# A pair's last six stack loads are issued from ScalarE's queue instead of SyncE's

## Chip, core and metric

The kernel runs on one core of a Trainium2 chip. The metric is the device time of one execution in microseconds (us). The core's engines each have an instruction stream of their own and meet only at semaphores: TensorE (PE, with its weight loads PEld), VectorE (DVE), ScalarE (ACT), GpSimd (POOL) and SyncE (SP), which here only issues DMAs. A row marked SPq or ACTq belongs to the instruction queue of that engine: a DMA that it issues, or a wait.

## What is computed

Two layers on x (32 batches, 64 tokens, 256 features). Each layer adds a gated attention and a gated feed-forward part. The time lies almost wholly in the first layer:

```
x = x + tanh(g_xattn[0]) * attention0(layernorm(x), ctx, ctx, mask)   # 8 heads of width 8, 256 x 256 scores, per batch
x = x + tanh(g_ffn[0])   * moe0(layernorm(x))                         # top-p router, 8 experts, 256 -> 512 -> 256, gate * up
x = x + tanh(g_xattn[1]) * attention1(layernorm(x), ctx, mask)        # one head, 64 tokens
x = x + tanh(g_ffn[1])   * moe1(layernorm(x))                         # 4 experts by token position
```

In attention0 a batch's x (64 x 256) is read as 64 channels by 256 positions: q = Wq x, k = Wk ctx, v = Wv ctx, and for each head softmax(q k / sqrt(8) + mask) v.

## The kernel before

The 32 batches are worked in 16 pairs. The main loop has 39 *steps* `n`, of which the first 32 hold the attention of one batch each; even and odd step make a pair `q = n // 2`. A step has eight *half steps* `i`, one for each head, and `g = 8n + i` numbers the heads through. Every engine's program is the same loop written out by hand in that engine's order, and the order in a half step is fixed.

The work of one head `g` runs through all engines. PE multiplies the stacked q and k into the scores (`scores`), DVE adds the mask and finds the row maximum (`maxima`, which ends with `exp_bias`, L1226), ACT takes the exponentials (`exps`, two ACTIVATEs at L701) and cuts them into a high f16 part (`p_high`, L709), POOL makes the low part (`p_low`, L592), SP issues one DMA that transposes both parts (`turn`, L429, into `p_turn`), and PE multiplies the turned parts with v (`times_v`), four half steps after the scores. Between these PE runs the experts of earlier pairs, one expert ("unit") in two half steps: gate matmuls in `psG`, up matmuls in `psU`; ACT takes a tanh of the gate (`unit_tanh`, L725), DVE multiplies, ACT cuts the product (`unit_high`, L731, into `hp_hi`), POOL makes its low part (`h_low`, L584, into `hp_lo`), and PE multiplies both with the down weights into `psY` (`unit_down`), one unit later. In half step 0 of an odd step ACT also turns out the normalised x of a finished pair (`x_high`, L715, into `xT`).

The scores need q and k as *stacks*: three bf16 parts of each, laid out several times over the partitions (`q_stack`, `k_stack`, double buffered by pair). The parts are stored to a scratch tensor in DRAM (`store_parts`, half step 3 of an even step) and read back by twelve DMAs for each pair, three in each of four *pieces*. `load_stacks(eng, par, q, piece)` issues one piece on the queue of the engine that it is given: L343, L348, and L353 or L356. It waits until the parts are stored. All twelve count on one semaphore, for which PE waits before the first scores of the next pair. Before, SP issues pieces 0 and 1 in half steps 6 and 7 of the even step and pieces 2 and 3 in half steps 0 and 1 of the odd step, each behind the turn of that half step. ACT issues pieces 2 and 3 for the very first pair alone, ahead of the loop.

SP's order in a half step is: the turn of head g-1 (which waits for `p_high` and `p_low` of that head), in half step 0 a mask load (L382), then a piece of stack loads where one is due. A turn that is ready is not issued before what stands ahead of it on SP.

Of the kernel before, what the change touches and what calls it, by code (L numbers as in the profile page):

```python
# [42 lines left out]
NPAIR = B * S // P  # L43
# [44 lines left out]
def build(nc, A, out):  # L88
# [5 lines left out]
    def sem(name):  # L94
        return ctx.enter_context(nc.semaphore(name))
# [7 lines left out]
    with ctx:  # L103
# [45 lines left out]
        s = {n: sem(n) for n in names}  # L149
# [183 lines left out]
        def load_stacks(eng, par, q, piece):  # L333

            eng.wait_ge(s["parts_stored"], 16 * (q + 1))
            if q < 2:
                eng.wait_ge(s["stacks_set"], 2)
                eng.wait_ge(s["q_zeroed"], q + 1)
            hh, i = piece // 2, piece % 2
            lo = 64 * hh  # L340
            src = [[part_d[par, w, c].rearrange("(g d r) n -> g d (r n)", g=2, d=DH)[hh]
                    for c in range(3)] for w in range(2)]
            eng.dma_start(  # L343
                q_stack[lo + 24 * i:lo + 24 * i + 24, par, hh, :, :, :].rearrange("r b h n -> r (b h n)"),
                src[0][i].unsqueeze(1).broadcast_to([DH, 3, 2048])
            ).then_inc(s[f"stack{par}_loaded"], 16)

            eng.dma_start(  # L348
                k_stack[lo + 24 * i:lo + 24 * i + 24, par, :, :, :].rearrange("r b h n -> r (b h n)"),
                part_d[par, 1].rearrange("c (g d r) n -> g d c (r n)", g=2, d=DH)[hh]  # L350
            ).then_inc(s[f"stack{par}_loaded"], 16)
            if i == 0:
                eng.dma_start(q_stack[lo + 48:lo + 56, par, hh, :, :, :].rearrange("r b h n -> r (b h n)"),  # L353
                             src[0][2]).then_inc(s[f"stack{par}_loaded"], 16)
            else:
                eng.dma_start(k_stack[lo + 48:lo + 56, par, :, :, :].rearrange("r b h n -> r (b h n)"),  # L356
                             src[1][0]).then_inc(s[f"stack{par}_loaded"], 16)
# [5 lines left out]
        def _(sp):  # L363
# [57 lines left out]
            def turn(g):  # L421

                sem, count = low_done(g)
                sp.wait_ge(s["phi_done"], g + 1)
                sp.wait_ge(sem, count)
                if g >= 4:
                    sp.wait_ge(s["pv_done"], g - 3)
                sem, count = turned(g)
                sp.dma_start(p_turn[:, g % 4, :, :, :, :].rearrange("p a t m n -> p (a t m) n"),  # L429
                             p_parts[:, g % 4, :, :, :].rearrange("p a t m -> p (a t m)"), transpose=True  # L430
                             ).then_inc(sem, 16)

            def step(n):
                q, par = n // 2, n // 2 % 2
                even = n % 2 == 0
                for i in range(8):
                    g = 8 * n + i
                    if 1 <= g <= 8 * B:
                        turn(g - 1)
                    if i == 0 and 1 <= n and n + 1 < B:  # L440
                        sp.wait_ge(s["max_done"], 16 * n)
                        load_mask(n + 1, (n + 1) % 2)
                    if even and i == 3 and 1 <= q and q + 1 < NPAIR:
                        sp.wait_ge(s[f"stack{1 - par}_loaded"], STACK_DMAS * 16 * ((q + 1) // 2))
                        store_parts(1 - par, q + 1)
                    if even and i == 2 and q + 3 < NPAIR:
                        sp.wait_ge(s["v_projected"], q + 2)
                        sp.dma_start(ctx_in[:, 1 - par, :], ctx_d[q + 3]).then_inc(s[f"ctx{1 - par}_loaded"], 16)
                    if even and i >= 6 and q + 1 < NPAIR:
                        sp.wait_ge(s["scores_done"], 8 * n)  # L450
                        load_stacks(sp, 1 - par, q + 1, i - 6)
                    if not even and i < 2 and q + 1 < NPAIR:
                        load_stacks(sp, 1 - par, q + 1, i + 2)
                    if i % 2 == 0 and 6 + g // 2 < 3 * NE:
                        load_weight_stage(6 + g // 2)
                    for t, r in late_at(n, i):
                        if r == 5 and t + 2 < ROUNDS:
                            load_late_ctx(t + 2)
                    out_group = group_at(Y_TURN_AT, g - 1)
                    if out_group is not None:  # L460
                        for tt in range(2):
                            store_out(2 * out_group + tt)
                    if (n, i) in ((TAIL_STEP, 4), (TAIL_STEP + 1, 0)):
                        load_late_weights(n - TAIL_STEP + 2)
                if n == TAIL_STEP - 2:
                    open_late()
                    for t in range(2):
                        load_late_ctx(t)
                if n == TAIL_STEP - 1:
                    for e in range(2):  # L470
                        load_late_weights(e)
# [174 lines left out]
        def _(act):  # L646
# [146 lines left out]
            def late_y_out(k):  # L793

                act.wait_ge(s["down_done"], 2 * (N_UNITS + 2 * k + 2))
                if k:
                    act.wait_ge(s["d_yT"], k)
                for hb in range(2):
                    act.activation(d_yT[:, hb, :].rearrange("p (r q e) -> p r q e", r=4, e=NE1),  # L799
                                   psY[:, hb, :].rearrange("p (e r q) -> p r q e", e=NE1, r=4),  # L800
                                   ACT.Copy, scale=dy_gate[:, 0:1]).then_inc(s["d_yevac"], 1)

            def step(n):
                q, tail = n // 2, tail_pair(n)
                for i in range(8):
                    g, hp, half = 8 * n + i, i // 2, i % 2
                    if 1 <= g <= 8 * B:
                        p_high(g - 1)
                    w = weight_at(g)
                    if w is not None:  # L810
                        w_high(*w)
                    if g < 8 * B:
                        exps(g)
                    k = group_at(Y_OUT_AT, g)
                    if k is not None:
                        late_y_out(k)
                    if half == 0:
                        u0 = unit_at(n, hp, 0)
                        if u0 is not None:
                            unit_tanh(u0)  # L820
                    else:
                        u1 = unit_at(n, hp, 1)
                        if u1 is not None:
                            unit_high(u1)
                    for t, r in late_at(n, i):
                        if r == -1:
                            late_norm(t, 0)
                        elif r == 5:
                            late_norm(t, 1)
                        elif r == 0:  # L830
                            late_copy("xn3T", t, x3T[:, :, :, :].rearrange("p u k t -> p (u k t)"), psT[:, :], "xt3_done")
                        elif r == 1:
                            late_copy("cxT", t, ctxT[:, :, :, :].rearrange("p u k t -> p (u k t)"),
                                      ps1[:, :, :].rearrange("p a b -> p (a b)"), "ctxT_done")
                        elif r == 2:
                            late_exps(t)
                        elif r == 3:
                            late_copy("pT_ready", t, pT[:, :, :].rearrange("p u t -> p (u t)"), ps1[:, 0, :], "pT_done")
                        elif r == 6:
                            late_x_high(t)  # L840
                    e = late_cut_at(n, i)
                    if e is not None:
                        late_w_high(e)
                    if tail is not None and (n % 2, i) == (0, 7):
                        norm2(tail)
                    if tail is not None and (n % 2, i) == (1, 0):
                        x_high(tail)
                    if (n % 2, i) == (1, 2) and q + 2 < NPAIR:
                        norm1(q + 2)
                    if tail is not None and (n % 2, i) == (1, 3):  # L850
                        route_exp(tail)
                    if (n % 2, i) == (1, 6) and q + 2 < NPAIR:
                        copy_qk(q + 2)
# [644 lines left out]
```

## Time and profile before

| | us |
|---|---|
| median of 3 runs (895.78 to 902.56) | 901.76 |
| the profiled execution's own time | 906.77 |
| its span, first to last instruction | 904.6 |
| PE busy | 785.4 (87%) |
| DVE busy | 685.6 (76%) |
| ACT busy | 611.2 (68%) |
| POOL busy | 589.3 (65%) |
| DMA queue of SP and ACT, share of the DMA engines | 69.3% |

The span has three stretches: a start of some 144 us in which the expert weights are prepared, the steady loop over the pairs to about 740 us, and the second layer. The page's chain that ended last covers only the end of the span, so the steady loop is read from waits and timelines. The profile's busy time of a queue's DMA row is the time of issuing it, and not of the transfer.

### The profile page before, as it was taken

How to read it: one execution, taken by the hardware profiler on the slowest of the kernel's cores; microseconds unless marked ns; L12 is line 12 of the kernel's file. 1: busy time of each engine (PE TensorE's matmuls, PEld its weight loads, DVE VectorE, ACT ScalarE, POOL GpSimd, SP SyncE). 2: the span in 40 equal slices, each digit the busy share in tenths (PEclk: the TensorE clock that was granted, in tenths of full speed). 3: DMA queues.
4: the chain of work that ended last, by engine and by line, in shares of the span. 5: the costliest groups of instructions: out<-in, count | busy, mean ns of one | idle time of the engine just before them, and what ended most of it. 6: DMA issues, size and time to landing. Idle time of an engine off the chain costs nothing. (4 is left out here: it accounts for less than half of the span.)

```text
span 904.6 us, 30146 instructions
## 1 busy us (share of the span) xinstructions
PE 785.4 (87%) x11511; PEld 726.2 (80%) x11511; DVE 685.6 (76%) x2353; ACT 611.2 (68%) x1330; POOL 589.3 (65%) x649
## 2 busy tenths in 40 slices
PE   3454679998999999989999999999998999878975
PEld 2333579898989898989898989888998999767975
DVE  3673768887888887888788888786887885766763
ACT  2374858777777777777677878776877774554552
POOL 4262737787869796969696878787887674233331
PEclk9655789999999999999999999999999999999999
DMA  6569998778788887787697878877779864110002
GB/s 222 168 145 207 235 225 188 130 142 148 135 154 139 147 148 136 145 136 150 129 151 148 157 132 155 135 156 122 158 146 138 136 111 126 48 60 12 26 1 95
DMA packets 319540, 122.99 MB, mean 136 GB/s; under 512 B 274716, under 2 KB 312612, under 8 KB 319396
## 3 DMA queue, kind: packets, MB, share of 16 engines
q1 hardware_dynamic: 318656, 120.53, 69.3%
q8 instruction: 91, 1.49, 0.7%
q10 hardware_dynamic: 740, 0.54, 0.2%
q14 instruction: 53, 0.43, 0.1%
HBM read 45.53 MB, written 8.39 MB: 60 GB/s over the span
## 5 line engine op out<-in xcount | busy, mean ns | idle before, releaser
L592 POOL TENSOR_TENSOR p_parts<-p,p_parts 128x512 f16<-128x512 f32 x256 | 297.1, 1160 | 158.0 <-ACT p_parts L709 147.3
L862 PE MATMUL psU<-xT,w_gu 128*128 128x128 f16 x3072 | 195.4, 221 | 8.3 <-DVE th_ga_h L1306 8.2
L862 PE MATMUL psG<-xT,w_gu 128*128 128x128 f16 x3072 | 195.8, 221 | 6.6 <-DVE th_ga_h L1298 6.1
L709 ACT ACTIVATE p_parts<-p 128x512 f16<-128x512 f32 x256 | 160.7, 628 | 46.5 <-DMA p_turn<-p_parts 45.8
L584 POOL TENSOR_TENSOR hp_lo<-th_ga_h,hp_hi 128x512 f16<-128x512 f32 x136 | 157.9, 1161 | 50.3 <-ACT hp_hi L731 46.4
L862 PEld LDWEIGHTS psG<-xT,w_gu 128*128 128x128 f16 x3072 | 178.5, 99 | 11.3 <-DVE th_ga_h L1298 9.0
L862 PEld LDWEIGHTS psU<-xT,w_gu 128*128 128x128 f16 x3072 | 178.5, 99 | 10.1 <-DVE th_ga_h L1306 9.5
L862 PE MATMUL psY<-w_dn,hp_hi 128*128 128x256 f16 x1024 | 183.0, 274 | 0.7 <-POOL hp_lo L584 0.7
L1222 DVE CUSTOM_DVE_ANT_0 ps<-ps,mask_in 128x256 f32<-128x256 f32 x256 | 104.2, 449 | 65.3 <-PE ps L862 64.4
L862 PE MATMUL psY<-w_dn,hp_lo 128*128 128x256 f16 x512 | 140.0, 273 | 0.0
L862 PEld LDWEIGHTS psV<-v_parts,p_turn 128*128 128x128 f16 x2048 | 87.7, 97 | 63.8 <-DMA p_turn<-p_parts 57.3
L701 ACT ACTIVATE p<-ps,exp_bias 128x256 f32<-128x256 f32 x256 | 106.9, 469 | 40.7 <-DVE exp_bias L1226 39.3
L862 PE MATMUL psV<-v_parts,p_turn 128*128 128x25 bf16 x2048 | 91.6, 175 | 47.4 <-DMA p_turn<-p_parts 45.2
L701 ACT ACTIVATE p<-psT,exp_bias 128x256 f32<-128x256 f32 x256 | 107.2, 472 | 37.3 <-DVE exp_bias L1226 30.1
L1222 DVE CUSTOM_DVE_ANT_0 psT<-psT,mask_in 128x256 f32<-128x256 f32 x256 | 103.7, 447 | 22.5 <-PE psT L862 22.4
L725 ACT ACTIVATE th_ga_h<-psG 128x512 f32<-128x512 f32 x136 | 80.9, 595 | 56.9 <-PE psG L862 55.1
L862 PEld LDWEIGHTS psY<-w_dn,hp_hi 128*128 128x128 f16 x1024 | 99.3, 99 | 14.4 <-POOL hp_lo L584 1.3
L1298 DVE SCALAR_TENSOR_TENSOR th_ga_h<-th_ga_h,psG 128x512 f32<-128x512 f32 x136 | 93.4, 687 | 8.7 <-ACT th_ga_h L725 7.9
L1306 DVE SCALAR_TENSOR_TENSOR th_ga_h<-psU,th_ga_h 128x512 f32<-128x512 f32 x136 | 92.0, 676 | 3.8 <-PE psU L862 2.7
L731 ACT ACTIVATE hp_hi<-th_ga_h 128x512 f16<-128x512 f32 x136 | 85.8, 631 | 8.2 <-DVE th_ga_h L1306 8.2
L1222 DVE DVE_READ_ACCUMULATOR2_ANT low_max<- 128x1 f32 x512 | 72.7, 142 | 0.0
L1316 DVE SCALAR_TENSOR_TENSOR x_res<-psY,tokw,x_res 128x256 f32<-128x256 f32 x128 | 60.8, 475 | 2.3 <-PE psY L862 2.2
(181 smaller groups left out, 1067.1 us busy)
## 6 DMA issues: line engine op xcount, KB each, us to landing
mask_in<-in_mask_Bx2048x_ff SPq DMA_DIRECT2D x32, 256.0 KB, 3.2
part_scratch<-parts SPq DMA_DIRECT2D x16, 384.0 KB, 3.9
q_stack<-part_scratch SPq DMA_DIRECT2D x62, 96.0 KB
k_stack<-part_scratch SPq DMA_DIRECT2D x62, 96.0 KB
stage<-in_L_ffn_gate_w SPq DMA_DIRECT2D x8, 512.0 KB, 5.5
stage<-in_L_ffn_up_w SPq DMA_DIRECT2D x8, 512.0 KB, 5.1
stage<-in_L_ffn_down_w SPq DMA_DIRECT2D x8, 512.0 KB, 4.8
p_turn<-p_parts SPq DMA_TRANSPOSE x256, 3.6
```

What stands on the lines that cost most here:

```text
L584: pool.tensor_tensor(hp_lo[:, u % 2, :], hb32[:, u % 2, :], hp_hi[:, u % 2, :], ALU.subtract).then_inc(s["h_split"], 1)
L592: pool.tensor_tensor(p_parts[:, g % 4, 1, :, :], p32[:, g % 2, :, :], p_parts[:, g % 4, 0, :, :], ALU.subtract).then_inc(s["plo_done"], 1)
L701: act.activation(p32[:, g % 2, nt, :], score_bank(g)[:, nt, :], ACT.Exp, bias=exp_bias[:, g % 2, nt:nt + 1], scale=-1.0).then_inc(s["exp_d ...
L709: act.activation(p_parts[:, g % 4, 0, :, :], p32[:, g % 2, :, :], ACT.Copy).then_inc(s["phi_done"], 1)
L725: act.activation(th, psG[:, :], ACT.Tanh, scale=0.5 * G_UNSCALE).then_inc(s["tanh_done"], 1)
L731: act.activation(hp_hi[:, u % 2, :], hb32[:, u % 2, :], ACT.Copy).then_inc(s["h_hi"], 1)
L862: return pe.matmul(out_, lhsT, rhs, start=start, stop=stop, skip_group_check=shares_bank)
L1222: dve.tensor_tensor_reduce(out=score_bank(g)[:, nt, :], in0=score_bank(g)[:, nt, :], in1=mask_in[:, n % 2, nt, :], scale=-1.0, scalar=HIGH ...
L1298: dve.scalar_tensor_tensor(out=ga, in0=th, scalar=1.0, in1=psG[:, :], op0=ALU.add, op1=ALU.mult).then_inc(s["gate_used"], 1)
L1306: dve.scalar_tensor_tensor(out=hb32[:, u % 2, :], in0=psU[:, :], scalar=0.5 * G_UNSCALE * G_UNSCALE, in1=ga, op0=ALU.mult, op1=ALU.mult).t ...
L1316: dve.scalar_tensor_tensor(out=x_res[:, row, :], in0=psY[:, y_bank(u), 0:D], scalar=tokw[:, row * NE + e:row * NE + e + 1], in1=x_res[:, r ...
```

## The change

In the loop of SP the two lines that load pieces 2 and 3 are taken out. In the loop of ACT three lines are put in: in half steps 0 and 1 of an odd step, behind the exponentials of that half step, ACT waits until the scores of the pair before last are done with the buffer, and issues the piece on its own queue. What is loaded, from where and to where, stays the same.

```
@@ block.sync, step(n)
                     if even and i >= 6 and q + 1 < NPAIR:
                         sp.wait_ge(s["scores_done"], 8 * n)
                         load_stacks(sp, 1 - par, q + 1, i - 6)
-                    if not even and i < 2 and q + 1 < NPAIR:
-                        load_stacks(sp, 1 - par, q + 1, i + 2)
                     if i % 2 == 0 and 6 + g // 2 < 3 * NE:
@@ block.scalar, step(n)
                     k = group_at(Y_OUT_AT, g)
                     if k is not None:
                         late_y_out(k)
+                    if n % 2 == 1 and i < 2 and q + 1 < NPAIR:
+                        act.wait_ge(s["scores_done"], 8 * (n - 1))
+                        load_stacks(act, (q + 1) % 2, q + 1, i + 2)
                     if half == 0:
                         u0 = unit_at(n, hp, 0)
```

SP's queue before, from the turn that follows piece 0 of a pair in the steady loop to the turns after piece 3:

```order
L429 DMA_TRANSPOSE p_turn<-p_parts 128x8x128
L343 DMA q_stack<-part_scratch 24x1x2048
L348 DMA k_stack<-part_scratch 24x1x2048
L356 DMA k_stack<-part_scratch 8x2048
L429 DMA_TRANSPOSE p_turn<-p_parts 128x8x128
L382 DMA mask_in<-in_mask_Bx2048x_ff 128x2x256
L343 DMA q_stack<-part_scratch 24x1x2048
L348 DMA k_stack<-part_scratch 24x1x2048
L353 DMA q_stack<-part_scratch 8x2048
L429 DMA_TRANSPOSE p_turn<-p_parts 128x8x128
```

The same place of SP's queue after the change:

```order
L429 DMA_TRANSPOSE p_turn<-p_parts 128x8x128
L343 DMA q_stack<-part_scratch 24x1x2048
L348 DMA k_stack<-part_scratch 24x1x2048
L356 DMA k_stack<-part_scratch 8x2048
L429 DMA_TRANSPOSE p_turn<-p_parts 128x8x128
L382 DMA mask_in<-in_mask_Bx2048x_ff 128x2x256
L429 DMA_TRANSPOSE p_turn<-p_parts 128x8x128 x8
```

Behind the mask load the turns now follow one another; before, one piece stood ahead of each of the next two.

ACT's queue before, from the end of an even step of the steady loop (the cut of the last head's exponentials) through half steps 0 and 1 of the odd step:

```order
L709 ACTIVATE p_parts<-p 128x512
L701 ACTIVATE p<-ps,exp_bias 128x256 x2
L725 ACTIVATE th_ga_h<-psG 128x512
L715 ACTIVATE xT<-psM 128x256
L709 ACTIVATE p_parts<-p 128x512
L701 ACTIVATE p<-psT,exp_bias 128x256 x2
L731 ACTIVATE hp_hi<-th_ga_h 128x512
```

The same place after the change, where ACT's lines stand two lines higher in the file (L699 for L701 and so on):

```order
L699 ACTIVATE p<-ps,exp_bias 128x256 x2
L343 DMA q_stack<-part_scratch 24x1x2048
L348 DMA k_stack<-part_scratch 24x1x2048
L353 DMA q_stack<-part_scratch 8x2048
L723 ACTIVATE th_ga_h<-psG 128x512
L713 ACTIVATE xT<-psM 128x256
L707 ACTIVATE p_parts<-p 128x512
L699 ACTIVATE p<-psT,exp_bias 128x256 x2
L343 DMA q_stack<-part_scratch 24x1x2048
L348 DMA k_stack<-part_scratch 24x1x2048
L356 DMA k_stack<-part_scratch 8x2048
L729 ACTIVATE hp_hi<-th_ga_h 128x512
```

Three DMA issues stand between the exponentials and the tanh of the gate, and three between the next exponentials and the cut of the unit's product.

## Rows read from the trace of the kernel before

**Rows 1.** The page: the span.
```profile
span 904.6 us, 30146 instructions
```

**Rows 2.** Waits, whole core, 144 to 740 us: line waited for, us, times, longest.
```profile
PE psV L862 <- DMA p_turn<-p_parts: 24.6, 21, 2.2
```

**Rows 3.** One source line, 144 to 740 us: count, duration ns min/median/max, starts.
```profile
L343 SPq DMA_DIRECT2D q_stack<-part_scratch x52: 683/695/1372, 161.3 to 694.7; - x52
```

**Rows 4.** Waits, whole core, 34 to 144 us.
```profile
PE psV L862 <- DMA p_turn<-p_parts: 20.6, 9, 6.4
```

**Rows 5.** Windows: length, busy PE, PEld, DVE, ACT, POOL, clock, DMA share, GB/s.
```profile
432.00:456.00 24.00, 22.11 (x323) 20.67 (x321) 16.91 (x67) 15.97 (x36) 16.24 (x16) 0.93 0.71 131
```

**Rows 6.** Timeline of SP, odd step around 430 us: start, us, instruction.
```profile
422.62 0.70 SPq L343 DMA_DIRECT2D q_stack<-part_scratch  x1
...
430.47 0.70 SPq L343 DMA_DIRECT2D q_stack<-part_scratch  x1
...
431.91 0.47 SPq L353 DMA_DIRECT2D q_stack<-part_scratch  x1
432.50 1.27 SPq L429 DMA_TRANSPOSE p_turn<-p_parts  x1
...
435.83 1.26 SPq L429 DMA_TRANSPOSE p_turn<-p_parts  x1
```

**Rows 7.** Timeline of PE, the same odd step; in brackets its idle time.
```profile
430.27 0.38 PE L862 MATMUL psY<-w_dn,hp_hi 128*128 128x256 f16 x2
...
431.24 1.50 PE L862 MATMUL psU<-xT,w_gu 128*128 128x128 f16 x24
...
435.21 0.38 PE L862 MATMUL psY<-w_dn,hp_hi 128*128 128x256 f16 x2
...
437.92 0.36 PE L862 MATMUL psV<-v_parts,p_turn 128*128 128x25 bf16 x8 [1.89 <-DMA p_turn<-p_parts]
438.13 2.61 PE L862 MATMUL psU<-xT,w_gu 128*128 128x128 f16 x24
```

**Rows 8.** Timeline of ACT, ahead of the loop: its own first piece and last.
```profile
22.11 0.77 ACTq L343 DMA_DIRECT2D q_stack<-part_scratch  x1
...
25.86 0.69 ACTq L356 DMA_DIRECT2D k_stack<-part_scratch  x1
```

**Rows 9.** Timeline of SP over the same time: its first and last stack load.
```profile
22.11 0.80 SPq L343 DMA_DIRECT2D q_stack<-part_scratch  x1
...
25.70 0.49 SPq L356 DMA_DIRECT2D k_stack<-part_scratch  x1
```

**Rows 10.** Timeline of ACT, half steps 0 and 1 of the odd step.
```profile
425.06 0.82 ACT L701 ACTIVATE p<-ps,exp_bias 128x256 f32<-128x256 f32 x2
425.77 0.59 ACT L725 ACTIVATE th_ga_h<-psG 128x512 f32<-128x512 f32 x1
426.50 0.38 ACT L715 ACTIVATE xT<-psM 128x256 f16<-128x256 f32 x1
...
428.02 0.64 ACT L731 ACTIVATE hp_hi<-th_ga_h 128x512 f16<-128x512 f32 x1
```

**Rows 11.** Source lines L699 and L714, single waits on ACT's queue, as in Rows 3.
```profile
L699 ACTq EVENT_SEMAPHORE  x1: 17/17/17, 424.1 to 424.1; - x1
L714 ACTq EVENT_SEMAPHORE  x1: 17/17/17, 425.1 to 425.1; - x1
L699 ACTq EVENT_SEMAPHORE  x1: 17/17/17, 426.8 to 426.8; - x1
```

**Rows 12.** Timeline of POOL, half step 1 of the odd step.
```profile
428.73 1.16 POOL L584 TENSOR_TENSOR hp_lo<-th_ga_h,hp_hi 128x512 f16<-128x512 f32 x1
```

**Rows 13.** Windows of 1 us in the odd step, as in Rows 5.
```profile
432.00:433.00 1.00, 1.00 (x18) 0.97 (x16) 0.56 (x5) 1.00 (x4) 1.00 (x1) 1.00 0.52 175
434.00:435.00 1.00, 1.00 (x22) 1.00 (x20) 1.00 (x4) 0.84 (x2) 1.00 (x2) 1.00 1.11 165
```

**Rows 14.** The turns (L429), 144 to 740 us: issue to landing.
```profile
DMA to landing us min/median/max: 3.0/3.5/6.1
```

More of the change, by code:

```diff
@@ L451, in step @@
                         load_stacks(sp, 1 - par, q + 1, i - 6)
-                    if not even and i < 2 and q + 1 < NPAIR:
-                        load_stacks(sp, 1 - par, q + 1, i + 2)
                     if i % 2 == 0 and 6 + g // 2 < 3 * NE:
@@ L816, in step @@
                         late_y_out(k)
+                    if n % 2 == 1 and i < 2 and q + 1 < NPAIR:
+                        act.wait_ge(s["scores_done"], 8 * (n - 1))
+                        load_stacks(act, (q + 1) % 2, q + 1, i + 2)
                     if half == 0:
```

## Prediction

> **What bounds the kernel now.** I read the page's shares first, then PE's waits in the steady stretch, then the timelines of SP, PE and ACT around one odd step. PE is busy for most of the steady stretch, so a gain has to come out of its idle time there, and nearly all of that has one name: it waits 24.6 us in 21 places for turned exponentials (`p_turn`) [rows 2]. The stretch holds 52 first issues of a piece [rows 3], four to a pair, so 13 pairs, and the wait is 24.6 / 13 = 1.9 us a pair.
>
> SP's timeline shows whom PE waits for [rows 6]. From 422.62 us on SP issues piece 0, a turn, piece 1, a turn, the mask and piece 2 with hardly a gap, and piece 2 takes from 430.47 to 431.91 + 0.47 = 432.38, or 1.91 us [rows 6]. The turn behind it goes out at 432.50, the next, behind piece 3, at 435.83, a distance of 3.3 us. PE's half step is shorter: the psY groups that begin at 430.27 and 435.21 are two half steps apart, 2.5 us each [rows 7]. So SP loses some 0.8 us in each half step with a piece. The turn of 432.50 releases PE at 437.92, after 1.89 us of idle time [rows 7]. Behind the wait 24 psU matmuls take 2.61 us where they took 1.50 [rows 7]: the clock has fallen to its lower level (1.2 of 2.4 GHz), and the 24 us around it have a mean granted clock of 0.93 [rows 5]. That is 24 x 0.07 = 1.7 us lost; two other steady windows of 24 us show the same, so 5 us in all.
>
> **What the change takes away.** SP loses two pieces, 2 x 1.9 us of issue, ahead of the two turns that are late. The first of them could go out where piece 2 stands now, at 430.47 instead of 432.50, if its head is ready, and the second some 3 to 4 us earlier. The late turn took 437.92 - 432.50 = 5.4 us from issue to PE; the range of landings is 3.0 to 6.1 [rows 14]. With 5.4 it lands at 435.9, and PE comes to it at 437.92 - 1.89 = 436.0. So I take the wait and its clock loss as gone, 24.6 + 5 = 29.6 us, and charge 0.4 us a pair for what is left of it, 5.2 us: all four pieces are now issued between 422.6 and 429, so the turns of that time share the DMA engines with more stack data. The bounds of this charge are 0 and the whole of the wait.
>
> In the start there are two more pairs with loads. PE waits 20.6 us there [rows 4]; the two odd steps are also runs of SP issues without a gap. There SP gives back at most 2 x 1.9 us in each, 7.6 us in both; other chains bind there too, and ACT has weights to cut, so the bounds are 0 and 7.6, and I take 4.
>
> **What the change adds.** ACT gets 3 + 3 DMA issues in each of 15 odd steps, and two waits. Neither wait is late: SP's piece 0 at 422.62 already passed the same count of stored parts and the same scores. The issues are not free. Ahead of the loop ACT issued the same two pieces: first start 22.11, last end 25.86 + 0.69 = 26.55, so 4.44 us, 2.2 us a piece [rows 8]. Queued behind the first piece are tanh and `x_high`, behind the second `unit_high`, then POOL's `h_low`, which PE's `unit_down` needs.
>
> What a piece costs depends on whether ACT's queue issues it while ACT still computes. Two timelines speak for that [rows 10, 11]. The wait at L714 belongs to `x_high` and stands behind both exponentials and the tanh. It passed at 425.1, when the first exponential had just begun (425.06) and the tanh was not to begin before 425.77. The wait at L699, which stands in front of the exponentials and behind the cut before them, passed at 424.1, a microsecond before they began. So ACT's queue runs ahead of the datapath by up to three ACTIVATEs, and is held only by a semaphore not yet there. No row shows a DMA issue doing so. I take it that it does:
>
> - first piece: starts 424.2, ends 424.2 + 2.2 = 426.4. The datapath is busy until 425.06 + 0.82 = 425.88. Tanh moves from 425.77 to 426.4, `x_high` from 426.50 to 426.9, the next exponentials by as much.
> - second piece: its exponentials' wait passes at 426.8 as now, so it runs from 426.8 to 429.0. `unit_high` moves from 428.02 to 429.0.
> - POOL's `h_low` begins 428.73 now, 0.07 us behind the end of `unit_high` [rows 10, 12]; it moves to 429.7 and ends 429.7 + 1.16 = 430.9. PE wants it at 430.27 [rows 7]. PE waits 0.6 us.
>
> Later ACT work moves with PE, so I count 0.6 us once a pair, 13 x 0.6 = 7.8 us. The bounds are 0 (a queue further ahead) and the whole issue in line. In line, both pieces delay `unit_high` by 2 x 2.2 = 4.4 us less the 0.4 us between the end of `h_low` (429.89) and 430.27, that is 4.0 us a pair. I choose near the lower end because three ACTIVATEs of lead are seen in exactly this place.
>
> In Perfetto Trace Analysis, "DVE / Act Engine Instruction", the Trainium skill says that the sequencer is free for the next instruction as soon as it has pushed an ACTIVATE into a wait queue. The trace agrees [rows 11]: a wait passes a microsecond ahead of the ACTIVATEs before it.
>
> **Sum.** Steady: 29.6 - 5.2 - 7.8 = 16.6 us. With the start's 4 it is 20.6 us off the profiled execution's 906.8 us (span 904.6 [rows 1] and 2.2 around it), 886.2. That execution is 5.0 us above the median of the runs, 901.8; taken from the median the sum gives 881.2 us. The last stretch has no loads and stays.
>
> **The rivals.**
>
> *ACT issues in line* (the other side). If a DMA issue waits until ACT is drained, or holds ACT's datapath, PE pays 4.0 us a pair instead of 0.6, 13 x 4.0 = 52 us against 29.6 + 4 gained: 18 us slower, 920; a wait of that length lowers the clock as that of 437.92 did, at up to 1.7 us each, so as far as 940. It decides from a price of 33.6 / 13 = 2.6 us a pair. For it: six plain issues ahead of the loop did keep ACT from computing for 4.4 us. Against it: nothing was queued there for ACT to compute, and the lead of the waits [rows 11].
>
> *One generator for both queues.* If issues of SP and ACT exclude one another, SP's turns wait for ACT's pieces, the lateness stays, and ACT's pieces wait for turns (1.27 us each [rows 6]) besides: nothing gained, 0.6 + 1.3 us paid, 13 x 1.9 = 25 us, 926. Ahead of the loop both queues issued six stack loads at once, SP from 22.11 to 25.70 + 0.49 = 26.19, 4.1 us for two pieces, where 2 x 1.9 = 3.8 are its price alone [rows 6, 8, 9]. So they overlap there; a transpose beside a load is not shown. The same page of the Trainium skill, "DMA Instruction — HWDGE", says that the generator of descriptors is shared by the two queues and locked for each issue; the two queues ahead of the loop do not show such a lock [rows 8, 9].
>
> *The transfers bind, not the issue.* If the DMA engines are full, an earlier issue does not land earlier, and PE's wait stays while ACT pays its 7.8 us: 901.8 + 7.8 - 4 = about 906. For it: the engines' share is 1.11 in one microsecond of the late stretch. Against it: it is 0.52 two microseconds earlier, and the turn was not yet issued then [rows 6, 13].
>
> **How the numbers follow.** The forecast has 0.62, in line 0.13, one generator 0.05, transfers bind 0.15, no ACT cost and no rest of the wait 0.05. The last gives 901.8 - 29.6 - 7.6 = 865. The range runs from 866 to 909: it takes in the transfers' rival and leaves out the two slower ones and the very end below. About 1% is what a measurement of this kernel can tell from no change, 9 us: faster means below 892.7, slower above 910.8. The forecast's own range is 866 to 898 (ACT's price up to 1.2 us, the rest of the wait up to 1 us a pair), of which about a tenth lies within 1%. So faster 0.61, same 0.20, slower 0.19.
>
> **What would show it.** Right: SP's turns in half steps 1 and 2 of an odd step follow the mask at once; PE's wait for `p_turn` in 144 to 740 us falls from 24.6 to below 6 us; ACTq rows of L343 start before the exponentials ahead of them have ended; PE waits about 0.6 us for `hp_lo` in half step 2. Wrong: these ACTq rows start only after the exponentials, or last over 1 us; PE's waits for `hp_lo` or `psG` reach 4 us; turns issued early still land late.

## The result and the profile after

| | before | after |
|---|---|---|
| median, us (lowest to highest, 4 runs each) | 902.16 (895.78 to 904.96) | 918.25 (912.59 to 924.26) |
| ratio, 95% interval | | 1.0195 [1.0155, 1.0236] |
| the profiled execution's own time, us | 906.77 | 924.26 |

The change makes the kernel about 2% slower; the prediction, 881 us with a range of 866 to 909, was on the wrong side. Lines of ACT stand two higher in the file of after, those of PE and DVE one lower.

The page of after, span and PE's busy time:

```profile
span 922.0 us, 30176 instructions
PE 794.0 (86%) x11511; PEld 727.5 (79%) x11511; DVE 690.0 (75%) x2353; ACT 607.8 (66%) x1330; POOL 588.3 (64%) x649
```

The span is 17.4 us longer than before [rows 1]. PE was busy for 794.0 instead of 785.4 us with the same 11511 matmuls, so 8.6 us are longer busy time and 8.8 us are idle time. Waits of PE in after, 144 to 740 us (line waited for, us, times, longest):

```profile
PE psV L863 <- DMA p_turn<-p_parts: 21.1, 17, 3.4
PE psY L863 <- POOL hp_lo L582: 7.9, 15, 1.0
PE psG L863 <- DVE th_ga_h L1299: 2.5, 3, 1.5
PE psG L863 <- DVE xT L1260: 1.1, 1, 1.1
```

The first row answers [rows 2]. The wait for turned exponentials, which was to go, fell from 24.6 to 21.1 us only, in fewer places (17 for 21) and longer ones (3.4 for 2.2 us). The next row is ScalarE's price. The start, 34 to 144 us, answers [rows 4]; nothing was gained there (20.6 before):

```profile
PE psV L863 <- DMA p_turn<-p_parts: 20.8, 8, 8.6
```

One odd step of after shows where the wait comes from now. SP's timeline (start, duration, us):

```profile
604.21 0.70 SPq L343 DMA_DIRECT2D q_stack<-part_scratch  x1
604.97 0.65 SPq L348 DMA_DIRECT2D k_stack<-part_scratch  x1
605.67 0.46 SPq L353 DMA_DIRECT2D q_stack<-part_scratch  x1
606.25 1.40 SPq L429 DMA_TRANSPOSE p_turn<-p_parts  x1
607.75 0.69 SPq L343 DMA_DIRECT2D q_stack<-part_scratch  x1
...
610.11 1.95 SPq L429 DMA_TRANSPOSE p_turn<-p_parts  x1
612.10 1.28 SPq L382 DMA_DIRECT2D mask_in<-in_mask_Bx2048x_ff  x1
613.50 2.38 SPq L429 DMA_TRANSPOSE p_turn<-p_parts  x1
```

The turn of 606.25 stands behind piece 0 as in before. No load stands between the mask and the turn of 613.50 any more. ACT at the same time:

```profile
605.12 0.69 ACTq L343 DMA_DIRECT2D q_stack<-part_scratch  x1
605.23 0.61 ACT L707 ACTIVATE p_parts<-p 128x512 f16<-128x512 f32 x1
605.75 0.45 ACT L699 ACTIVATE p<-ps,exp_bias 128x256 f32<-128x256 f32 x1
605.84 0.69 ACTq L348 DMA_DIRECT2D k_stack<-part_scratch  x1
606.11 0.46 ACT L699 ACTIVATE p<-ps,exp_bias 128x256 f32<-128x256 f32 x1
606.57 0.50 ACTq L353 DMA_DIRECT2D q_stack<-part_scratch  x1
607.11 0.60 ACT L723 ACTIVATE th_ga_h<-psG 128x512 f32<-128x512 f32 x1 [0.55 <-issue]
```

ACT's piece 2 starts at 605.12, before the exponentials that stand ahead of it (605.75 and 606.11) have run: the queue runs ahead of the datapath, as the prediction took it to. So the loads of piece 2 go out at 605.12 to 607.07, while those of SP's piece 0 (604.21 to 606.13) are in flight, and the turn of 606.25 comes in between. The *landing* of a turn is from here on the time from its issue to its last byte. For the turn of 606.25 alone the profile gives:

```profile
DMA to landing us min/median/max: 9.5/9.5/9.5
```

In the same place of before (the turn issued at 424.7, behind piece 0) the same line says 3.8 us. Here the turn lands at 606.25 + 9.5 = 615.75, and PE, which had done with what it had at 612.48, waits for it:

```profile
612.21 0.27 PE L863 MATMUL psY<-w_dn,hp_lo 128*128 128x256 f16 x1
615.84 0.39 PE L863 MATMUL psV<-v_parts,p_turn 128*128 128x25 bf16 x8 [3.35 <-DMA p_turn<-p_parts]
```

Over the whole stretch the landing of turns has the median 3.6 us and the maximum 10.3, against 3.5 and 6.1 [rows 14]. A wait of this length costs twice, since the granted clock is low behind it. Windows of after (length; PE, PEld, DVE, ACT, POOL busy; then the granted clock, the share of the DMA engines, GB/s), first the idle stretch, then the three stretches of the steady loop at the low level:

```profile
613.00:615.00 2.00, 0.00 (x0) 0.00 (x0) 0.03 (x1) 0.00 (x0) 0.00 (x0) 0.94 0.82 169
570.40:573.80 3.40, 3.40 (x34) 2.91 (x32) 1.70 (x8) 2.19 (x7) 2.81 (x3) 0.50 1.32 173
614.80:621.60 6.80, 5.76 (x62) 5.27 (x63) 2.26 (x11) 3.51 (x9) 3.43 (x3) 0.50 0.87 177
662.50:669.40 6.90, 5.82 (x62) 5.32 (x63) 2.32 (x11) 3.51 (x9) 3.42 (x3) 0.51 0.78 173
```

The same three stretches of before:

```profile
353.00:356.40 3.40, 3.40 (x28) 3.00 (x27) 1.16 (x2) 0.57 (x3) 0.97 (x1) 0.50 1.16 163
438.30:441.70 3.40, 3.40 (x30) 3.09 (x28) 0.38 (x3) 2.05 (x5) 2.94 (x3) 0.50 1.03 194
615.80:619.20 3.40, 3.40 (x30) 3.03 (x28) 0.67 (x3) 1.10 (x3) 0.48 (x1) 0.50 0.85 158
```

The low level, 1.2 GHz, holds for 17.1 us in after and for 10.2 in before. Half of that is lost: 8.5 us against 5.1.

### The profile page after: what moved, and what is told of

Its sections match the earlier page's. It is cut to its first block and busy times, and to the rows that moved or that the text cites. A ratio compares the mean times of both kernels' runs of the same rounds, so it can differ in the third digit from the quotient of the medians.

```text
span 922.0 us, 30176 instructions
## 1 busy us (share of the span) xinstructions
PE 794.0 (86%) x11511; PEld 727.5 (79%) x11511; DVE 690.0 (75%) x2353; ACT 607.8 (66%) x1330; POOL 588.3 (64%) x649
## 5 line engine op out<-in xcount | busy, mean ns | idle before, releaser
L863 PE MATMUL psU<-xT,w_gu 128*128 128x128 f16 x3072 | 197.6, 222 | 8.2 <-DVE th_ga_h L1307 8.2
L863 PEld LDWEIGHTS psU<-xT,w_gu 128*128 128x128 f16 x3072 | 180.3, 99 | 10.2 <-DVE th_ga_h L1307 9.3
L699 ACT ACTIVATE p<-ps,exp_bias 128x256 f32<-128x256 f32 x256 | 106.5, 468 | 58.8 <-DVE exp_bias L1227 55.1
L699 ACT ACTIVATE p<-psT,exp_bias 128x256 f32<-128x256 f32 x256 | 107.2, 472 | 52.2 <-DVE exp_bias L1227 34.2
```

The source lines that it names most:

```text
L699: act.activation(p32[:, g % 2, nt, :], score_bank(g)[:, nt, :], ACT.Exp, bias=exp_bias[:, g % 2, nt:nt + 1], scale=-1.0).then_inc(s["exp_d ...
L863: return pe.matmul(out_, lhsT, rhs, start=start, stop=stop, skip_group_check=shares_bank)
```

## The experiments

Theory, formed from this profile: SP issues its turns early enough, but stack loads on ACT's queue share the DMA engines with SP's queue, and a turn between them lands about 3 us later. Rivals: ACT's own price is the loss; SP's lateness was never the cause of the wait before; the loads now merely come too close together, whatever the queue (all twelve go out in 6.6 us on the mean, where before they took 13.8).

The table joins all runs (medians in us, ratios against the kernel before on the same chip, which gave 897.5 to 900.7 us there; PE's waits are those of 144 to 740 us).

| run | median | ratio, 95% interval | p_turn | hp_lo | stacks |
|---|---|---|---|---|---|
| before | 902.16 | | 24.6 | none | |
| after | 918.25 | 1.0195 [1.0155, 1.0236] | 21.1 | 7.9 | |
| e1, before, pieces 2 and 3 with 1/16 of the bytes | 894.85 | 0.9945 [0.9914, 0.9976] | 19.0 | 0.8 | |
| e2, after, ACT's pieces with 1/16 of the bytes | 883.20 | 0.9817 [0.9767, 0.9867] | none | 13.1 | |
| e9, after, SP's pieces with 1/16 of the bytes | 885.07 | 0.9849 [0.9809, 0.9890] | 0.7 | 11.9 | |
| e3, ACT's pieces in odd 2 and 4 | 912.41 | 1.0154 [1.0113, 1.0196] | 16.0 | 3.1 | |
| e12, ACT's pieces in odd 3 and 5 | 891.91 | 0.9921 [0.9883, 0.9960] | 5.1 | 7.5 | 2.6 |
| e11, ACT's loads one by one | 897.04 | 0.9983 [0.9960, 1.0006] | 9.9 | 1.8 | |
| e8, all four pieces on ACT | 902.06 | 1.0033 [0.9999, 1.0066] | none | 22.8 | |
| e4, all on SP, spread | 889.35 | 0.9872 [0.9831, 0.9913] | 2.3 | 1.0 | 10.0 |
| e5, as e4, last two on ACT | 911.54 | 1.0136 [1.0080, 1.0192] | 8.1 | 4.2 | |
| e7, all on SP, two later | 881.00 | 0.9799 [0.9745, 0.9853] | 6.0 | 1.0 | |
| e6, all on SP, finer | 877.63 | 0.9770 [0.9717, 0.9823] | none | 0.7 | 6.9 |
| e10, as e6, a half step earlier | 874.59 | 0.9727 [0.9683, 0.9772] | 4.4 | 0.7 | |

And the landing of the turns by the half step in which SP issues them, in us: means worked out from the trace over the 13 pairs of the steady stretch. A turn counts as landed with the last of the 16 counts on its buffer's semaphore; the few turns with fewer counts in the trace are left out.

| | even 6 | even 7 | odd 0 | odd 1 | odd 2 | odd 3 | odd 4 |
|---|---|---|---|---|---|---|---|
| before | 3.5 | 3.8 | 3.8 | 4.1 | 3.9 | 3.8 | 3.9 |
| after | 3.4 | 7.0 | 6.8 | 6.4 | 4.9 | 4.1 | 3.7 |
| e2, ACT's pieces cut | 3.5 | 3.9 | 4.1 | 4.2 | 3.9 | 3.6 | 3.6 |
| e9, SP's pieces cut | 3.3 | 5.5 | 5.0 | 4.6 | 4.0 | 3.9 | 3.7 |
| e4, all on SP | 3.6 | 3.9 | 3.7 | 4.1 | 4.1 | 4.0 | 4.0 |
| e5, ACT in odd 2, 4 | 3.4 | 4.0 | 3.6 | 5.4 | 5.8 | 6.3 | 5.6 |
| e3, ACT in odd 2, 4 | 3.4 | 3.7 | 5.0 | 6.1 | 6.5 | 6.0 | 5.5 |
| e12, ACT in odd 3, 5 | 3.4 | 3.8 | 4.2 | 5.2 | 6.2 | 5.5 | 6.0 |
| e8, all on ACT | 4.7 | 4.3 | 5.5 | 6.2 | 4.4 | 3.8 | 3.8 |
| e11, one by one | 3.4 | 4.7 | 5.1 | 5.4 | 5.8 | 5.6 | 5.1 |

The half step named for ACT is the place in its program; its queue runs ahead, so the loads go out earlier.

### e1 and e2: the bytes of pieces 2 and 3

Before (e1) and after (e2), with 128 of 2048 elements of each row in these pieces; all issues stay. The rest of q and k is left out, and the scores are not those of the whole data.

```
+            wide = 128 if q and piece >= 2 else 2048
-                src[0][i].unsqueeze(1).broadcast_to([DH, 3, 2048])
+                src[0][i][:, 0:wide].unsqueeze(1).broadcast_to([DH, 3, wide])
```

> The kernel before, with the loads of pieces 2 and 3 of pairs 1 to 15 cut to 128 of 2048 elements a row: SP issues as many loads at the same places, but 15/16 of their bytes are left out (so the scores of those rows are not computed from the whole data). If the wait for the turned exponentials in before comes from SP issuing late (the prediction's reading), the turns stay as late, the wait in 144 to 740 us stays between 18 and 25 us, and the time stays within 5 us of 902. If it comes from stack transfers that share the DMA engines with the turns, the landing of the late turn falls from 5.4 to about 3.3 us, the wait falls below 8 us, and the time to 870 to 885.

> The changed kernel with the same cut: ACT issues pieces 2 and 3 at the same places, with 15/16 of their bytes left out. It shows the price of the issues on ACT without their transfers. If the transfers are what went wrong with the change, the wait for turned exponentials nearly goes (below 6 us in the steady stretch), the wait of PE for hp_lo stays (about 8 us, 0.6 a pair), and the time is 875 to 888. If ACT's delay is what went wrong and the late turns follow from it, the time stays above 905.

PE's waits in e1 and then in e2:

```profile
PE psV L863 <- DMA p_turn<-p_parts: 19.0, 21, 2.1
```

```profile
PE psY L864 <- POOL hp_lo L583: 13.1, 14, 2.0
PE psG L864 <- DVE xT L1261: 1.9, 2, 1.2
PE psG L864 <- DVE th_ga_h L1300: 1.4, 2, 0.8
```

In e1 the wait of before stays in its 21 places (19.0 for 24.6 us) though the bytes are gone: most of it is SP's issue, as the prediction read it. A smaller part is bytes: the time is 5.8 us below before on the same chip, a little more than the 5 expected. In e2 no wait for `p_turn` is left, and the turns of even 7 to odd 1 land in 3.9 to 4.2 us. So the bytes that ACT's queue moves are needed for the new wait; ACT's issues alone do not make it. ACT's price shows alone there: 13.1 / 13 pairs = 1.0 us a pair, above the 8 us expected. That 883.2 us is close to the 881 of the forecast is luck in part: the forecast had 5.2 for the rest of the wait and 7.8 for ACT, 13.0 in all, and e2 pays 13.1 for ACT alone.

### e9: the bytes of SP's pieces

> The changed kernel, in which SyncE's pieces 0 and 1 of pairs 1 to 15 carry 128 of 2048 elements of each row (q and k of those pairs are therefore not filled); ScalarE's pieces 2 and 3 carry all. The issues stay as in the changed kernel, the stack bytes are on ScalarE's queue alone. If a turn is late whenever ScalarE's queue moves stacks: the turns of odd half steps 0 to 2 still land in 5.5 us or more on the mean, PE's wait for p_turn is 10 us or more, 900 to 912 us. If it takes stack bytes on both queues at once: landings below 4.8 us on the mean, wait for p_turn below 5 us, PE's wait for hp_lo about 13 us as in the version with ScalarE's bytes cut, 880 to 888 us.

```
+            wide = 128 if q and piece < 2 else 2048
```

PE's waits in e9:

```profile
PE psY L864 <- POOL hp_lo L583: 11.9, 14, 2.1
PE psG L864 <- DVE th_ga_h L1300: 1.4, 2, 0.8
PE psG L864 <- DVE xT L1261: 1.1, 1, 1.1
PE psV L864 <- DMA p_turn<-p_parts: 0.7, 1, 0.7
```

Here ACT's loads are whole and SP's are nearly empty, and the wait is gone as well. The landings are 5.5, 5.0 and 4.6 us in even 7 to odd 1, above the 3.8, 3.8 and 4.1 of before but below the 7.0, 6.8 and 6.4 of after. So ACT's bytes alone make about half of the delay (1.7 of 3.3 us in even 7), and it takes stack bytes of both queues to make a turn so late that PE waits in this place.

### e4 and e5: the same places, another queue

Pieces in even half step 6 and odd 0, 2 and 4: all on SP (e4), or the last two on ACT (e5).

```
-                    if not even and i < 2 and q + 1 < NPAIR:
-                        load_stacks(sp, 1 - par, q + 1, i + 2)
+                    if not even and i in (0, 2, 4) and q + 1 < NPAIR:
+                        load_stacks(sp, 1 - par, q + 1, 1 + i // 2)
```

> The kernel before, with SP issuing all four pieces, one in every second half step: half step 6 of the even step and 0, 2 and 4 of the odd step. ACT issues none in the loop. SP then needs 2 turns and one piece in two half steps, 4.5 of 5 us, so it does not fall behind, and the transfers are spread. If the wait in before is SP's backlog or bunched transfers, it falls below 8 us and the time to 870 to 885. If the total of bytes and not their place binds, the wait stays above 18 us and the time within 8 us of 902.

> Pieces 0 and 1 on SyncE (even half step 6, odd 0), pieces 2 and 3 on ScalarE (odd 2 and 4): it differs from the spread version that gave 889.35 us (PE wait for p_turn 2.3 us in 144 to 750) only in the queue of the last two pieces. Sharing theory (loads on a second queue delay the turns on the first): the turns of odd half steps 2 to 5 land in 5 us or more on the mean instead of 4, PE's wait for p_turn comes back to 10 to 18 us, the time is 902 to 912. Bunching theory (too many stack bytes too early, whatever the queue): landings and wait stay as in the spread version (2 to 4 us), the time is 889 plus ScalarE's price of 0 to 0.6 us a pair, 889 to 898.

PE's waits in e4:

```profile
PE ps L862 <- DMA k_stack<-part_scratch: 10.0, 10, 1.9
PE psV L862 <- DMA p_turn<-p_parts: 2.3, 4, 1.1
```

and in e5:

```profile
PE psV L865 <- DMA p_turn<-p_parts: 8.1, 10, 2.3
PE psU L865 <- DVE th_ga_h L1309: 7.1, 10, 1.4
PE psG L865 <- DVE th_ga_h L1301: 6.0, 9, 1.5
PE psY L865 <- POOL hp_lo L584: 4.2, 12, 1.0
```

In e4 the pieces are two half steps apart, so SP catches up after each, and a turn lands as in before. The price is a new wait for the stacks, because the last piece goes out late; so the time lies above the 870 to 885 expected. In e5 the turns of odd 1 to 4 land in 5.4 to 6.3 us instead of 4.0 to 4.1. The queue is not all that differs: since ACT's queue runs ahead, piece 2 goes out 3.3 us ahead of the turn of odd 2 on the mean, where in e4 it goes out 1.5 us behind it, and it starts while SP still issues piece 1. And the expected 10 to 18 us of wait for `p_turn` did not come, only 8.1. The larger part of the new idle time has another cause: in an even half step the tanh of a unit stands behind ACT's piece, DVE's product waits for it, and PE's `psG` and `psU` for that (13.1 us together). So e5 shows sharing, an earlier issue and ACT's price in one.

### e3 and e12: ACT's two pieces later

The two lines of ACT in the changed kernel, with `i in (2, 4)` (e3) or `i in (3, 5)` (e12) instead of `i < 2`.

> The changed kernel, with ACT's pieces at half steps 2 and 4 of the odd step instead of 0 and 1; all data is loaded. The transfers of pieces 2 and 3 then come after those of pieces 0 and 1, about when SP issued them before. If bunched transfers delayed the turns, landings go back to 6 us at most, the wait for turned exponentials falls below 10 us, hp_lo costs up to 1 us a pair, and the time is 880 to 895. If two queues that take turns on each DMA engine delay a turn whenever ACT's loads are under way, the wait stays at 20 us or more, and the time at 910 to 920.

> The changed kernel with ScalarE's two pieces in odd half steps 3 and 5 instead of 0 and 1: SyncE's stack loads have landed by then, and behind a piece stands the cut of a unit's product, not the tanh. If turns are late only where stack bytes of both queues are in flight at once: turns land within 5 us on the mean in all half steps, the wait for p_turn in 144 to 740 us is below 5 us, hp_lo costs some 13 us, 880 to 890 us. If loads on the second queue delay the turns beside them by themselves: odd half steps 3 to 6 land in 5.5 us or more on the mean, the wait for p_turn is 8 us or more, 895 to 912 us.

PE's waits in e12:

```profile
PE psY L863 <- POOL hp_lo L582: 7.5, 18, 1.6
PE psV L863 <- DMA p_turn<-p_parts: 5.1, 6, 2.3
PE ps L863 <- DMA k_stack<-part_scratch: 2.6, 3, 1.9
```

e12 is faster than before where after is slower, by 2.7% between their ratios: the same six loads on the same queue, three and four half steps later. Yet neither expectation holds whole. In all 13 pairs SP's last stack packet ends 2.8 to 5.9 us before ACT's first one starts, and still the turns of odd 2 to 4 land in 5.5 to 6.2 us: a load on the second queue delays the turn beside it by about 2 us on its own, with three loads in flight; beside a piece on SP's own queue the turns of before land in 4.1 us at most on the mean. PE waits for that 5.1 us only.

In e3 SP's stack packets are gone too before ACT's start (by 0.4 to 3.4 us), and the turns land as late as in e12; but the wait is 16.0 us, 14.4 of it for the turns of odd 0 and 1. What differs is how late SP issues. The time from the end of POOL's part of a head to the issue of its turn is 1.8 and 2.1 us on the mean for these two in e3, and 1.9 to 2.3 us for even 7 to odd 1 in after. For odd 3 and 4 in e12 it is 1.0 and 0.3 us. So PE loses time where both come together: a turn that SP issues about 2 us late, behind pieces of its own, and ACT's loads beside it. Behind ACT's pieces in e3 stands the tanh besides, as in e5 (`psG` 4.9 and `psU` 3.8 us).

### e8 and e11: all on ACT, or one by one

In e8 SP's two lines are gone too, and ACT issues pieces 0 and 1 in even half steps 6 and 7. In e11 ACT's six loads of after are spread singly over odd half steps 0 to 4.

```
-                        load_stacks(sp, 1 - par, q + 1, i - 6)
+                    if n % 2 == 0 and i >= 6 and q + 1 < NPAIR:
+                        act.wait_ge(s["scores_done"], 8 * n)
+                        load_stacks(act, (q + 1) % 2, q + 1, i - 6)
```

> All four pieces on ScalarE's queue, in even half steps 6 and 7 and odd 0 and 1; SyncE issues only turns and masks there. Sharing theory (a stack load on the second queue delays the turns on the first): the turns of even half step 7 to odd 2 land in 6 us or more on the mean, PE's wait for p_turn stays at 15 us or more although SyncE is never late, and ScalarE's price is doubled: 918 to 935 us. If a turn was late because both queues held stack loads at the same time, and not because the second queue did: landings near 4 us, wait for p_turn below 6, and with ScalarE's price of some 1 to 2 us a pair 885 to 900.

> Pieces 0 and 1 on SyncE as in the changed kernel, ScalarE's six loads one by one in odd half steps 0 to 4 (two in the last). If what counts is how many stack bytes of both queues are in flight together: landings of odd half steps 0 to 4 stay below 5 us on the mean, wait for p_turn 2 to 8 us, and with a smaller price on ScalarE 880 to 892 us. If any load on the second queue delays the turn beside it: landings of 5.5 us or more over all five half steps, wait for p_turn 10 us or more, 902 to 915 us.

PE's longest wait in e8:

```profile
PE psY L863 <- POOL hp_lo L579: 22.8, 28, 1.6
```

In e8 the whole gain on `p_turn` (24.6 us) is paid back in `hp_lo`, 22.8 / 13 = 1.75 us a pair, and the time is that of before. The sharing theory in its plain form (a turn is late whenever the second queue has loads, and PE waits) falls here: no wait for `p_turn` is left, although the turns of odd 0 and 1 land in 5.5 and 6.2 us. Nothing but the mask stands ahead of SP's turns there, and these two go out 0.1 and 0.3 us behind POOL's part; they have landed 2.1 and 1.5 us before PE takes them. PE also comes later for them, having waited for `hp_lo`; how much each saves was not separated. e11 lies between its two expectations: landings of 4.7 to 5.8 us from even 7 to odd 4, 9.9 us of wait, the time of before.

### e7, e6 and e10: no second queue

e7 puts pieces 2 and 3 of SP in odd half steps 1 and 3. e6 and e10 break the pieces up, so that SP issues single loads; e10 by

```
+        STACK_AT = {(0, 6): (0, 1, 2), (0, 7): (3, 4), (1, 0): (5,), (1, 1): (6, 7), (1, 2): (8, 9), (1, 3): (10, 11)}
```

where (1, 2) is odd half step 2 and the numbers are loads in their old order. e6 has 2, 2, 1, 2, 2, 2 and 1 loads and ends in odd 4.

> All on SyncE: pieces 0 and 1 in even half steps 6 and 7 as before, pieces 2 and 3 in odd 1 and 3. Issue theory: two pieces in a row cost SyncE 2 x 0.8 us of lateness, odd 0 without a piece gives it back; the wait for p_turn falls from 24.6 to 4 to 10 us, the wait for stacks to below 4 us, 882 to 893 us. Bytes theory: the wait stays above 15 us, 896 to 902.

> All twelve loads on SyncE's queue, in two, two, one, two, two, two and one DMAs over seven half steps, so that no half step holds a whole piece. If SyncE's issue is all that made the turns late: PE's wait for p_turn stays at or below 3 us in 144 to 750, and the wait for the stacks (10.0 us where the last piece went out in odd half step 4) shrinks to below 6 because only one DMA is left there; 878 to 887 us. If it is the number of stack bytes in flight behind a turn: wait for p_turn 10 us or more, 892 to 900.

> All on SyncE as in the fine version (877.6 us; its wait for the stacks is 6.9 us), in 3, 2, 1, 2, 2 and 2 DMAs, so that the last goes out a half step earlier. If the stack wait is only the late last load: it falls below 2 us, the wait for p_turn stays below 4 us, 869 to 876 us. If two DMAs in each of three half steps make the turns late again: wait for p_turn 5 us or more, 877 to 884 us.

PE's waits in e10:

```profile
PE psV L864 <- DMA p_turn<-p_parts: 4.4, 5, 1.6
PE psG L864 <- DVE th_ga_h L1300: 0.8, 1, 0.8
PE psY L864 <- POOL hp_lo L586: 0.7, 2, 0.5
```

e7 and e6 come out up to a microsecond below the times that the issue theory gave (882 to 893 and 878 to 887), e10 within its own (869 to 876). The stack wait of e6, 6.9 us, was to be below 6; a half step earlier, in e10, it is gone, for 4.4 us of wait for `p_turn`, which was to stay below 4. The gain that the prediction sought was there, without ScalarE: with room between the loads, SP's turns go out late (4.3 us behind POOL's part in odd 4 of e10, on the mean) but land in about 4 us, mostly in time for PE. e10, at 874.59 us (0.9727), is the fastest kernel of the study and beats both.

The last rival, loads too close together whatever the queue, is not wholly excluded: no run issues twelve loads on SP's queue as densely as after does. It cannot be all, since in e3, e11 and e12 the loads are spread out (13 to 17 us from first to last) and turns still land 2 us late.

## Why the prediction was wrong

**Right: what bounds.** The wait of before is mostly SP's late issue (e1), its lower clock included. Taken away on SP's own queue, in e10, it gives 24.5 us, start included, against the 29.6 that the sum put on the wait and its clock.

**Right: SP is relieved.** The turns of odd 1 and 2 went out 4.2 and 5.5 us behind POOL's part in before, and PE waited for them 24.0 of its 24.6 us. In after they go out 2.3 and 1.9 us behind it, and PE waits for them 2.9 us.

**Right: ACT's queue runs ahead.** The piece of 605.12 starts before the exponentials ahead of it. So the rival of an issue in line (2.6 us a pair and more) fell. The price of 0.6 us a pair is 7.9 / 13 = 0.6 in after, but there PE is already late for `p_turn`, and the match is luck; alone it is 0.9 to 1.0 (e9, e2), 4 to 5 us more than the 7.8 of the sum. A piece took less to issue than the 2.2 us assumed: 605.12 to 607.07, 1.95 us.

**Wrong: "With 5.4 it lands at 435.9".** This is the step that failed. The landing of a turn was carried over from before, where everything ahead of it stood on the same queue, and the charge for sharing was set at 0.4 us a pair. The bound named beside it, the whole of the wait, was the right end. Measured, the turns of even 7 to odd 1 land 2.3 to 3.3 us later (7.0, 6.8, 6.4 for 3.8, 3.8, 4.1). PE waits 21.1 / 13 = 1.6 us a pair, and for other turns than before: 18.3 of the 21.1 us are for those of even 7 and odd 0, behind pieces 0 and 1, which still go out about 2 us late. In the step shown it is the one behind piece 0, where before it was the one behind piece 2 [rows 6, 7].

**Wrong by it: the clock.** The 5 us that were to come back are there in before (5.1). Instead the low level costs 8.5 us in after, 3.4 more, with single waits of up to 3.4 us and the low level behind them, as at 615 us. In e2, without the wait, the steady stretch has no low clock, and the page gives PE 778.6 us of busy time for the same 11511 matmuls, below the 785.4 of before. Where the rest of the 8.6 us of longer busy time in after comes from was not found.

**Not gained: the start.** 4 us were taken, the wait there is 20.8 against 20.6. The same loads collide there too: the turns of even 7 in the two pairs of the start land in 10.6 and 11.0 us, where before it was 5.8 and 7.3.

The sum with measured terms: the `p_turn` wait 3.5 us less, `hp_lo` 7.9 more, `psG` 2.5 + 1.1 for 0.4, so 3.2 more, PE's busy time 8.6 more, the start 0.2 more: 16.4 us of the 17.4 by which the span grew.

**The rivals.** By the number alone the rival of an issue in line (920) is nearest to 918.25, and that is luck, since its mechanism fell. No lock of the length of an issue was seen: ACT's 26 issues of L343 take 674 to 703 ns in after, where SP issues beside them, and single later loads of a piece take up to 1.25 us, against 1.99 on SP before. The turns did take longer to issue at times (up to 4.5 us, against 2.7 before); why was not found. The rival of the transfers (906) came nearest in its mechanism: an earlier issue did not land earlier, the wait stayed and ACT's price came on top. Its reading that the turn was not yet issued in the microsecond with 0.52 was loose, since the turn of 432.50 goes out in it [rows 6, 13]. And it spoke of full engines. They were not filled by bytes: e4 moves all of them with landings near 4 us. The packets tell what changed (queue: packets, MB, share of 16 engines). From 606.3 to 615.8 us in after, from the issue of the turn to its landing:

```profile
q1 hardware_dynamic: 1820, 0.80, 82.1%
q10 hardware_dynamic: 160, 0.46, 20.2%
```

and in the 9.5 us of before from 424.6 to 434.1, from the issue of its turn on:

```profile
q1 hardware_dynamic: 2749, 1.44, 71.9%
```

q1 is SP's queue (so the 69.3% of the first table is SP's alone), q10 ACT's. A packet of q1 takes 0.821 x 16 x 9.5 us / 1820 = 69 ns in after and 0.719 x 16 x 9.5 / 2749 = 40 ns before, with less data moved in all (1.26 for 1.44 MB). By size, the packets of 256 bytes, of which the turns consist, took about 64 ns on the mean instead of 28, those of the stacks (4096 bytes) 219 instead of 203. The Trainium skill says of this, in DMA: Bandwidth & Descriptors, "Issuing engines are not separate DMA queues", that DMAs of several engines run interleaved on the same 16 DMA engines, and that issuing from several saves only time on the sequencer. The runs agree in both halves: e2 has the saving (883.2 us), and in after the two queues together take 102% of the 16 engines' time in these 9.5 us. "Queues, rings and completion order" on the same page of the Trainium skill says that a DMA engine takes turns between the queues that have work for it, a whole packet at a time (there a bundle of descriptors, which need not be what the profile counts as one). That fits a turn behind piece 0 that waits for piece 2 as well, but no run here shows the order within an engine.

**What stays open.** ACT's loads lengthen a turn by about 2 us on their own (5.5 us in even 7 of e9, 5.5 to 6.2 in e12) and by some 3 us beside SP's loads; that the wait of after needs bytes of both queues is shown, what happens within a DMA engine is not. Nor was a smaller packet size on ACT's queue tried.

## What to carry to other kernels

A load moved to a second queue is no longer ordered behind the first queue's transfers but runs among them: price it by the landing of what it now overlaps, not by the landing seen when all stood in one queue. If the trouble is that several issues stand in a row ahead of an urgent one, try first to spread them on the queue that has them; here that gained 2.7%, and the second queue lost 2%. An early issue only helps if the transfer keeps its duration, so read issue-to-landing beside issue time.

## What was not expected of the hardware

With 1/16 of the bytes the issue of a first load takes as long: medians of 700 and 694 ns for pieces 2 and 3 on SP in e1, the same as in before. Two queues that each move a moderate load can make a transpose take 10.3 us where the same bytes in one queue did not take it above 6.1 in the steady stretch [rows 14].
